# Queries and keys of the attention in two float32r parts on halves of the array, and the first image's operands copied by selection matmuls

## The reference, cut to what matters

```python
xin = jnp.einsum('nchw,oc->nohw', x, W_in) + b_in[None, :, None, None]
q = _conv(query, Wq[idx], 'SAME').reshape(n, HEADS, HC, -1)     # 4 heads, 8 channels, 1024 queries
k = _conv(token, Wk[idx], 'VALID').reshape(n, HEADS, HC, -1)    # 900 keys
v = _conv(token, Wv[idx], 'VALID').reshape(n, HEADS, HC, -1)
w = jax.nn.softmax(jnp.einsum('nhcq,nhcd->nhqd', q, k), axis=-1)
a = jnp.einsum('nhcd,nhqd->nhcq', v, w)
```

## Time and profile before

| | us |
|---|---|
| device time, median of 3 runs | 351.98 (349.85 to 353.33) |
| device time of the profiled execution | 355.27 |
| its span, first to last instruction | 353.3 |
| TensorE busy | 314.1 (89%) |
| VectorE busy | 218.1 (62%) |
| ScalarE busy | 176.2 (50%) |
| mean granted clock of TensorE | 0.936 |

### The profile page before, as it was taken

The page is one execution under the profiler, slowest core; times in us unless marked ns, Lnnn a source line. Parts: engine busy times, 40 slices in busy tenths (PEclk is TensorE's granted clock), DMA queues, the critical chain, the costliest instruction groups (busy, mean ns, idle before and its releaser), DMA issues. The chain is left out here.

```text
span 353.3 us, 6973 instructions
## 1 busy us (share of the span) xinstructions
PE 314.1 (89%) x2780; PEld 119.5 (34%) x2787; DVE 218.1 (62%) x484; ACT 176.2 (50%) x338; POOL 35.6 (10%) x42
## 2 busy tenths in 40 slices
PE   5899887999845799999999999999998998895894
PEld 2578332334211222332323233233331222443831
DVE  3990435674845228686878868887773123489945
ACT  1210110251833658787888878879786684300000
POOL 8300000100000000100101001010100105306000
PEclk9999999999955569999999999999998899999999
DMA  7100000037875313003030030000000000000001
GB/s 243 42 4 4 12 0 3 0 86 193 160 93 152 113 45 122 0 3 120 2 100 21 3 120 2 1 2 2 1 2 1 1 2 0 0 2 1 4 2 59
DMA packets 4043, 15.21 MB, mean 43 GB/s; under 512 B 955, under 2 KB 1771, under 8 KB 3083
## 3 DMA queue, kind: packets, MB, share of 16 engines
q1 hardware_dynamic: 4011, 14.76, 15.4%
HBM read 12.21 MB, written 2.37 MB: 41 GB/s over the span
## 5 line engine op out<-in xcount | busy, mean ns | idle before, releaser
L677 ACT ACTIVATE arena_b<-ps 128x512 f32<-128x512 f32 x232 | 125.4, 605 | 41.6 <-PE ps L1164 40.6
L1140 PE MATMUL ps<-arena_a 72*128 72x450 bf16 x256 | 90.2, 384 | 6.2 <-issue 4.7
L1164 PE MATMUL ps<-arena_a 75*128 75x512 bf16 x224 | 87.1, 400 | 7.3 <-DMA arena_a<-mt_sb 6.5
L884 DVE TENSOR_REDUCE mx<-ps 128x1 f32<-128x450 f32 x120 | 69.2, 617 | 6.7 <-PE ps L1140 5.7
L879 DVE CUSTOM_DVE_ANT_0 sums<-ps,relus 128x450 bf16<-128x450 f32 x68 | 41.6, 625 | 46.6 <-PE ps L1140 35.8
L1182 PE MATMUL ps<-arena_b,vt 128*32 128x512 f32 x448 | 62.8, 634 | 0.5 <-ACT arena_b L677 0.4
L1164 PEld LDWEIGHTS ps<-arena_a 75*128 75x128 bf16 x224 | 22.0, 100 | 81.6 <-ACT arena_b L677 44.8
L685 ACT ACTIVATE relus<-ps 128x450 f32<-128x450 f32 x68 | 37.3, 551 | 11.5 <-PE ps L1140 11.5
L1140 PEld LDWEIGHTS ps<-arena_a 72*128 72x128 bf16 x256 | 24.5, 102 | 41.5 <-issue 12.7
L1031 PE MATMUL ps<-arena_a,cst 32*32 32x512 f32 x864 | 28.6, 596 | 1.3 <-ACT arena_a L628 1.3
L1001 PE MATMUL ps<-zeros 128*128 128x512 bf16 x82 | 21.3, 398 | 6.7 <-DMA xa<-x 3.8
(11 more groups left out here) (139 smaller groups left out, 229.3 us busy)
## 6 DMA issues: line engine op xcount, KB each, us to landing
arena_b<-wmodes SPq DMA_DIRECT2D x4, 1024.0 KB, 4.9
arena_a<-k_scratch SPq DMA_DIRECT2D x3, 516.8 KB
arena_a<-q_scratch SPq DMA_DIRECT2D x3, 384.0 KB
cst<-consts SPq DMA_DIRECT2D x1, 1045.0 KB, 9.0
k_scratch<-arena_b SPq DMA_DIRECT2D x3, 344.5 KB, 3.8
cst<-consts SPq DMA_DIRECT2D x1, 864.5 KB, 6.9
arena_a<-k_scratch SPq DMA_DIRECT2D x6, 129.2 KB
arena_a<-k_scratch SPq DMA_DIRECT2D x3, 258.4 KB
```

The source lines that it names most:

```text
L677: nc.scalar.activation(probs[:, n % PRING, :], ps[:, SCORE_RING[n % len(SCORE_RING)], :], ACT.Exp).then_inc(expd, 1)
L884: nc.vector.tensor_reduce(mx[:, a, e:e + 1], bank, AX.X, ALU.max).then_inc(max_read, 1)
L1140: mm(ps[:, block_bank(i), 0:KHALF], qst[0:PAIR_ROWS, e, g, qt * P:(qt + 1) * P], kst[0:PAIR_ROWS, g, at:at + KHALF], start=True, stop=True ...
L1164: last = mm(ps[:, bank, :], kst[0:S_ROWS, g, t * P:(t + 1) * P], qst[0:S_ROWS, e, g, :], start=True, stop=True)
```

## The change

K and Q are held in two float32r parts (the value rounded, and the rest) instead of three bfloat16 parts: 2 x 2 pairs of parts x 8 channels are 32 rows, with one row of zeros 33, with two rows for the maximum 35. A head lies on one half of the array's rows: heads 0 and 2 on rows 0 to 34, heads 1 and 3 on rows 64 to 98 (`ROW_TILE` = 64). In the plan blocks of the two heads of a pair alternate.

For the first image, first half of the queries, the stacks are not fetched through DRAM: 8 "replica" items (four for each pair of heads: two for K's halves, one for its difference, one for Q) each multiply the two parts with 0/1 matrices (`select`, 32 x 128) into PSUM, and ScalarE or VectorE copies the bank into the stack. All other stacks still go through DRAM, now in float32. Those of Q and the transfers of the maxima move from SyncE's queue to GpSimd's; `mt_sb` goes out in two DMAs.

The second half of Q's convolution, V's convolution and V's turning move behind the first blocks: two items of the stream follow each of their 12 pieces. The window path moves into half 2. Half 1 now has only 6 pairs of 16 with `diff`. The left-over keys of the four heads are laid out by GpSimd (`rest_tiles`) so that two accumulating matmuls of 128 rows replace four of 32 columns. Blocks have 4 banks (3 to 6) throughout, outputs one (7). `FIRST_AHEAD` 18 becomes 16, `BLOCKS_PER_STEP` 4.15 becomes 4.5. The matmuls on zeros at the very start change from 6 full ones, 3 float32r ones and 16 on quarters of the rows to 16 full ones; those ahead of the attention (`keep_clock(2, 3)`) are dropped. `maps`, `xm` and everything after the attention stay.

```diff
-PARTS = 3
-PAIR_ROWS = PARTS * PARTS * HC
-S_ROWS = PAIR_ROWS + PARTS
+PARTS = 2
+SLOTS = G // 2
+ROW_TILE = P // 2
+STACK = PARTS * PARTS * HC
+M_ROW = STACK + 1
+MAX_ROWS = STACK + 1
+S_ROWS = M_ROW + PARTS
-MAX_RING = (3, 4, 5)
-O_RING = (6, 7)
+MAX_RING = (3, 4, 5, 6)
+O_RING = (7,)
-FIRST_AHEAD = 18
-BLOCKS_PER_STEP = 4.15
+FIRST_AHEAD = 16
+BLOCKS_PER_STEP = 4.5
+STEP = 's0 X s1 X s2 X V s3 X'
+REST_STEP = 's0 X V'
+REPLICAS = [(what, j, n, engine) for j in range(2)
+            for what, n, engine in (("k", 0, "act"), ("q", 0, "dve"), ("k", 1, "act"), ("k", 2, "dve"))]
+ORDER_OF_MAX = [(2 * j + u) * HALF_TILES + qt for j in range(2) for qt in range(HALF_TILES) for u in range(2)]
+WINDOW_AT = {(2, 5): "mean", (2, 9): "value", (2, 13): "gate"}
+PAIRED = (0, 3, 6)
+    early = [("conv", "q", 1, px) for px in range(3)] + [("qsplit",)]
+    early += [("conv", "v", e, px) for e in range(2) for px in range(3)] + [("vcopy",), ("vt", 0), ("vt", 1)]
+    take(4 + 2)
+    for item in early:
+        plan.append(item)
+        take(2)
+    take(len(REPLICAS) + 2 * ROWS_OF_MAX + 1 + FIRST_AHEAD - 6 - 2 * len(early))
...
             sp.wait_ge(kd_written, PARTS * 16)
-            stack_k(0, 0, HEADS // 2)
-            sp.wait_ge(qd_written[0], PARTS * 16)
-            stack_q(0, 0, 0, HEADS)
-            stack_k(1, HEADS // 2, HEADS)
+            stack_k(0, 2, 4)
...
+            def stack_q(i, e, s0, s1):
+                for u in range(2):
+                    for v in range(PARTS):
+                        src = q_dram[v, e].rearrange("c (s u) n -> u c s n", u=2)[u][:, s0:s1]
+                        for t in range(PARTS):
+                            r0 = ROW_TILE * u + HC * (PARTS * v + t)
+                            pool.dma_start(qst_f[r0:r0 + HC, e, s0:s1, :], src).then_inc(q_in[i], 16)
+            pool.wait_ge(xin_ready, 2)
+            pool.wait_ge(qd_written[0], PARTS * 16)
+            stack_q(0, 0, 2, 4)
+            stack_q(1, 0, 4, 6)
...
+                if item[0] == "turn":
+                    pool.wait_ge(*blocks_read[item[1]])
+                    for u in range(2):
+                        pool.dma_start(qst_f[r0:r0 + PARTS, e, 2 * b:2 * b + 2, :].rearrange("p s n -> p (s n)"),
+                                       mt_f[n * u:n * (u + 1), :]).then_inc(m_in, 16)
+                    if s == 0:
+                        pool.wait_ge(m_in, 2 * 16)
+                        stack_q(2, 0, 6, SLOTS)
+                        pool.wait_ge(qd_written[1], PARTS * 16)
+                        stack_q(3, 1, 0, SLOTS)
+                    if 1 <= s < B:
+                        rest_tiles(s)
...
+            def replica(i, what, j, n):
+                bank = ring_bank(i)
+                r = images[0]
+                if what == "k":
+                    pe.wait_ge(k_low, n + 1)
+                    for u in range(PARTS):
+                        last = mm(ps[:, bank, 0:KHALF], select[r, 0, j, u], kparts[r, u, K_RANGES[n]],
+                                  start=(u == 0), stop=(u == 1))
...
-                mm(ps[:, block_bank(i), 0:KHALF], qst[0:PAIR_ROWS, e, g, qt * P:(qt + 1) * P],
-                   kst[0:PAIR_ROWS, g, at:at + KHALF],
+                j, u = divmod(h, 2)
+                r = slice(ROW_TILE * u, ROW_TILE * u + MAX_ROWS)
+                mm(ps[:, bank, 0:KHALF], qst[r, e, 2 * b + j, qt * P:(qt + 1) * P], kst[r, 2 * b + j, at:at + KHALF],
                    start=True, stop=True).then_inc(max_scored, 1)
...
-                    last = mm(ps[:, bank, :], kst[0:S_ROWS, g, t * P:(t + 1) * P], qst[0:S_ROWS, e, g, :],
+                    r = slice(ROW_TILE * u, ROW_TILE * u + S_ROWS)
+                    last = mm(ps[:, bank, :], kst[r, 2 * b + j, t * P:(t + 1) * P], qst[r, e, 2 * b + j, :],
                               start=True, stop=True)
...
-            keep_clock(7, 6)
-            for _ in range(3):
-                mm(ps[:, 7, 0:KHALF], zeros_r[:, 0:P], zeros_r[:], start=True, stop=True)
+            keep_clock(7, 16)
```

More of the change, by code:

```diff
@@ L142, in attention_plan, with put @@
     stream, i = [], 0
-    for s in range(2 * B):
[L144 to L150, removed]
+    def put(kind, *rest):
+        nonlocal i
+        stream.append((kind, i, *rest))
+        i += 1
+    for r in REPLICAS[:4]:
+        put("replica", *r)
+    group = []
+    for s in range(2 * B):
+        for p, a in enumerate(ORDER_OF_MAX):
+            if s == 0 and p == 4:
+                for r in REPLICAS[4:]:
+                    put("replica", *r)
+            kinds = ("diff", "first") if s < 1 or p % 8 in PAIRED else ("first", "second")
+            group.append([("max", s, a, kind) for kind in kinds])
+            if p % 2:
+                for items in (zip(*group) if INTERLEAVE else group):
+                    for item in items:
+                        put(*item)
+                group = []
+            if (s, p) in WINDOW_AT:
+                put("window", WINDOW_AT[(s, p)])
         stream.append(("split", s))
-        stream.append(("turn", i, s))
-        i += 1
+        put("turn", s)
     for at in [at for at, item in enumerate(stream) if item[0] == "turn"]:
@@ L173, in attention_plan @@
         for t in range(DT + 1):
-            units = HEADS if t < DT else 1
+            pattern = (STEP if t < DT else REST_STEP).split()
+            n0 = s * EXP_UNITS + t * HEADS
             due += BLOCKS_PER_STEP * (1.0 if t < DT else 0.6)
[L176 to L183, removed]
+            taken = places = 0
+            for what in pattern:
+                if what[0] == "s":
+                    plan.append(("score", n0 + int(what[1])))
+                elif what[0] == "V":
+                    if prev:
+                        plan.append(("values", *prev, what[1:]))
+                else:
+                    places += 1
+                    k = int(due * places / pattern.count("X") + 1e-6)
+                    take(k - taken)
+                    taken = max(taken, k)
             due -= taken
@@ L194, in attention_plan @@
             step += 1
-    plan += [("values", *prev)] + [item for _, item in later]
+    plan += [("values", *prev, "")] + [item for _, item in later]
     plan += [("read", prev[0]), ("write", prev[0])]
@@ L433, in build @@
                 split_after[item[1]] = vector_reads
-            elif item[0] == "turn" or (item[0] == "max" and item[4] != "diff"):
+            elif item[0] in ("window", "turn") or (item[0] == "max" and item[4] != "diff"):
                 vector_reads += 1
@@ L533, in _ @@
[L533 to L545 removed]
+            sp.wait_ge(pattern_set, 1)
```

659 lines of the change are left out of this document (379 added, 280 removed).

## The result

| | before | after |
|---|---|---|
| device time, median (4 runs each, taken together) | 352.65 (349.85 to 353.78) | 438.72 (433.88 to 439.71) |
| profiled execution and its span | 355.27, 353.3 | 437.79, 435.8 |
| TensorE busy | 314.1 (89%) | 406.5 (93%) |
| VectorE busy | 218.1 (62%) | 222.1 (51%) |
| ScalarE busy | 176.2 (50%) | 171.7 (39%) |

What follows compares the result with a forecast made beforehand. Bounds: transfers from 89 to 117 us, TensorE at 1.2 GHz to about 131, then at full clock to about 267. 11.3 + 3 + 16.8 - 8.0 - 2 = 21.1 off 351.98 gives 331 (profiled 334.2); range 312 to 346.

Steps and rivals of the forecast that it cites:

- The steady stretch at the full clock: Attention after the early low-clock stretch: TensorE at full clock, halves of 20.2 instead of 21.3 us; gain 16.8.
- a rival at 0.12: Clock falls in the steady stretch: low steps 3.8 us, 1.15 more; 30 of 48 give 365; chance 0.12.
- a sign against itself: Granted-clock row of the page: more than one 5 beyond 130 us would show the forecast wrong.
- The halves of the array: Score and block pairs: forecast 0.33 us together; rival, halves don't work together, step 3.8, 386 us, chance 0.08.
- First score: Start of the attention: first score at 106 us, bounds 102 to 114, against 117.3; gain 11.3.
- GpSimd's DMAs: Transfers of Q's stacks ahead of the maxima's: 1.05 us each for 16; rival, late, 341 us, chance 0.1.
- The stretch at 1.2 GHz: Around the first score: clock falls again for some 13 us of steps, costing 5 instead of 8; gain 3.
- The step: Steady attention step: 2.66 us instead of 2.80 on average, bounds 2.45 to 2.80; a half 20.2.
- The likeliest case: The forecast itself: TensorE, VectorE and ScalarE level at 2.3 to 2.4, step 2.66, 331 us; chance 0.35.
- the rival at 0.2: Steady step: VectorE and ScalarE set it, it stays at 2.80 us, total 338; chance 0.2.
- The tail: After the last block: grows from 34 scores to 47, 3.25 steps of 2.45 us; loss 8.0.
- The start of half 1, the rest tiles, the fills: Counted at nothing: fills hidden in a 6.64 us wait, rest units under 0.5; uncovered, half 1 up to 5 late.

Runs made afterwards that it cites:

- bf16: Changed kernel with blocks and scores reading the upper 16 bits of their float32r stacks as bfloat16, still 33 and 35 rows: 389.52 us.
- blocks64: Changed kernel with 64 rows for the blocks of maxima alone, scores kept at 35 rows: 378.14 us.
- rows64: Changed kernel with blocks and scores on all 64 rows of their half, added rows zeros: 346.09 us, kernel before 348.64.
- rows64_t: The 64-row changed kernel again, timed in rounds against the kernel before: 348.29 against 353.28 us, ratio 0.988.
- rows64_warm: 64-row kernel plus one matmul on zeros ahead of each of blocks 20 to 57, before the first score: 355.41 us, ratio 1.015 to the kernel before.
- rows64_bf16: 64-row kernel with blocks and scores read as bfloat16 (upper 16 bits, lower precision): 337.32 us.
- rows64_ring4: 64-row kernel with four banks for scores and three for blocks instead of three and four: 359.0 us, ratio 1.014 to the kernel before.
- before35: Kernel before, bfloat16, with blocks on 33 rows instead of 72 and scores on 35 instead of 75: 485.76 us, kernel before 348.64.

## Why the prediction was wrong

**The steady stretch at the full clock: the step that failed.** The sum kept the stretch from 130 us on at the full clock and put the fall there into a rival at 0.12, argued from gaps: "it works 2.39 of 2.66 by its own sequence". The fall came, and for another reason. The change halves the rows of each block and score, and the runs show that this is enough to bring the low level and more rows enough to end it: 33 and 35 rows in the old kernel take 486, and back at 64 rows the new one takes 346, at 48 rows 357. The type counts as well (bf16), and in blocks64 and bf16 the same rows stood at both levels; by what measure the level is set stays open. The prediction looked only at when TensorE is busy, never at how much of the array a matmul fills; `72*128` stood in its rows, and 33 and 35 in the text of the change.

Its argument against the fall was misread, too: "in the tail it kept 1.00 at gaps of a similar size". That holds from 278 us on the earlier trace rows. Just behind the last block the kernel before fell to 0.50 as well, with TensorE nearly full (columns as in the earlier trace rows); in the earlier trace rows it is the two slices at 8:

```profile
271.00:277.00 6.00, 5.86 (x22) 1.52 (x19) 0.00 (x0) 3.00 (x6) 0.00 (x0) 0.50 0.01 2
```

What it named as a sign against itself, more than one 5 in the clock row beyond 130 us, is what the page shows.

**The rival's price.** A low step was put at 3.8, 1.15 more than a full one; most take 4.44 and the short ones 4.06, where rows64 has 2.81 and 2.61. That is 1.63 and 1.45 more, and over the 38 steps of five halves it makes up the 62.2 us between the two kernels. The rival took 30 of 48 steps at that level and gave 365; all 48 at its price would give 386. Nearly all were low: the five whole halves took 172.4 instead of 103 forecast (2 of it for the window path), 69 of the miss. The low stretch around the first score, some 13 us in the sum, lasted from 106 to 222.

**The halves of the array** work together (starts within 0.01, pairs 0.32 at the full level against 0.33 forecast). That rival is out. Its price was wrong as well: the 0.336 of a whole array is not what such a load takes at the full level. There it is 0.19 whatever the rows, 0.18 to 0.19 for 33, 35 or 64 and this for the 128 of a rest unit in rows64:

```profile
L1292 PEld LDWEIGHTS ps<-qst,krest x16: 186/188/189, 129.9 to 285.9; 128*128 128x128 f32 x16
```

At 0.50 loads take 0.28 to 0.33. With 0.19 the rival's step would be 8.5 x 0.19 + 0.99 = 2.6 instead of 3.8, an estimate.

**What the rest of the change is worth** is read from rows64, where the clock is as forecast. Its profiled execution has 346.1 where the sum had 334.2, so 12 of the 21 us of gain weren't there either. By the timed runs more is lacking: the sum starts from an execution of 355.27, and side by side with the kernel before rows64_t gains only 353.28 - 348.29 = 5.0. Against the sum's own terms:

- *First score*: 109.19, forecast 106: a gain of 8.1, not 11.3. The first block went at 77.95 (77.4 forecast). GpSimd's DMAs cost 0.57 each, not 1.05, and were out by 93; that term was too dear, yet it decided nothing: the maxima were turned only at 103.32, 5 us later than the sum's 98, behind VectorE, which is busy 9.69 of 10 us from 99 on, and their DMA was issued at 105.69. The transfer had landed at 108.46, after 2.8 (3 forecast), and the score went 0.7 later, behind the blocks ahead of it.
- *The stretch at 1.2 GHz*: about 14 us around the first score. Half 0 took 27.5, where 20.2 with 1.5 for its end and 5 for the clock makes 26.7. Against a half of 21.8 the clock's part is 27.5 - 21.8 - 1.5 = 4. The size came near, in part by luck: only 7 us of the stretch lie behind the first score, not 13, and rows64_warm, at the full level there, still takes 26.0, so that the low level itself is worth some 1.5 of the half.
- *The step*: 21.8 for a half, not 20.2. The likeliest case said that level loads would still give 0.14 a step; the rival at 0.2, VectorE and ScalarE set the step, was the better reading for the full clock (338 with it)., which the prediction read as bearing out a rule on tiled arrays, come from a kernel whose blocks and scores go one at a time. The run rows64_bf16 shows how a shorter pair does move the half, to 20.5, so TensorE is part of the chain, and rows64_ring4 that its waits only move from one ring to the other. The window of rows64 from 200 to 220 has TensorE, VectorE and ScalarE all near their end (columns as in the earlier trace rows):

```profile
200.00:220.00 20.00, 19.57 (x113) 7.83 (x117) 16.77 (x40) 17.05 (x35) 2.20 (x3) 1.00 0.01 2
```

  The sum had taken TensorE's share as 2.39 of a step without the waits that the order of its queue brings. The five halves of rows64 take 110.2, where the sum had 5 x 20.2 and 2 for the window path: 7.2.
- *The tail*: three steps at 256.88, 259.49 and 262.09, so 2.60 each, not 2.45: 0.15 for some 11 steps, 1.6 us.
- *The start of half 1, the rest tiles, the fills*: nothing of them is seen in rows64.

So 3.2 of the start, 0.8 of half 0, 7.2 of the halves and 1.6 of the tail make 12.8, where rows64 lacks 11.9. The changed kernel's profiled execution is 437.8 - 334.2 = 103.6 above the sum: 91.7 went with the added rows and the clock, 12 are these.

## What to carry to other kernels

When a change cuts a contraction into fewer rows, expect TensorE's clock to be at stake even if the matmuls follow each other without a gap, and read the granted clock together with the rows of the matmuls. Rows of zeros are a cheap cure: pairs are 0.31 to 0.32 apart at the full level with 64 rows too, so they cost no time on the array, and here were worth 92 us. Judge a trick for the clock by the end of the next stage and not by the clock: keeping it full with matmuls that aren't hidden lost 10 us at the start, and the half behind it was 1.5 shorter.

## What the runs showed of the hardware

- Rows that hold only zeros count for the clock: with 29 or 31 of them added to each matmul the mean granted clock was 0.956, without them 0.696.
- The clock can stay at 1.2 GHz for 310 us (before35, from 94 to 404), with TensorE busy 10.00 of 10 in the windows read between 124 and 390.
- The level is not a function of the rows alone: blocks of 64 rows beside scores of 35 ran at 0.50 for 54 us and then at 1.00 for 110 (blocks64), and 33 and 35 rows in bfloat16 at 0.50 from 100 to 243 us and then at 1.00 for 48 us (bf16).
- A load of 128 columns of float32r weights takes 0.18 to 0.19 us at 1.00 for 33, 35, 64 and 128 rows (after, rows64), 0.28 to 0.33 at 0.50 (after); in bfloat16 0.10 (rows64_bf16, 64 rows).
- Two matmuls of 450 and 512 columns on two halves of the rows, with new weights each: 0.32 a pair in float32r, 0.21 in bfloat16; at 1.2 GHz 0.42 to 0.55 in float32r. One between them on all rows takes part in no pair: 0.32 more.
- GpSimd issues a DMA in 0.57 us (16 in 9.11), less than the 0.69 of SyncE for stacks of the same operand.
- Values in two parts of 256 columns cost 2 x 0.57, in one of 512 0.99.
